# Two transformer layers on one core: attention blocks in another order, half 1's third stage on GpSimd inside the attention, half 0's second norm and router inside it too, and another order of VectorE at both hand-overs

## The reference

```python
x = x + two_graph_attention_layers(ctx_512, layernorm(x))        # adjacency from x
x = x + experts(layernorm(x))          # 8 experts, 2 per row, 256 -> 512 -> 256
x = x + (1 - gamma) * layernorm(x) + gamma * symmetric(sigmoid(sim) * top_76(sim))
h = layernorm(x)
r = rmsnorm(h, ln1)                                              # in layer L1_ffn
q, k, v = rope(r @ Wq), rope(r @ Wk), r @ Wv                     # 32 heads, 4 for k and v, of 128
y = h + (softmax(causal(q @ k.T / sqrt(128))) @ v) @ Wo
t = rmsnorm(y, ln2)
w = top 8 of 32 of sigmoid(t @ Wr) + bias, normalised scores
x = x + y + sum_e w[e] * (silu(t @ Wg[e]) * (t @ Wu[e])) @ Wd[e] + shared_expert(t)
```

## Time and profile before

| what | value |
|---|---|
| median of 3 runs (lowest to highest) | 1194.25 us (1194.03 to 1195.7) |
| the profiled execution | 1188.88 us |
| its span | 1187.1 us |
| TensorE busy | 1062.9 us, 90% of the span |
| VectorE busy | 876.8 us, 74% |
| ScalarE busy | 595.0 us, 50% |
| GpSimd busy | 381.0 us, 32% |
| mean granted clock | 0.922 of full |

### The profile page before, as it was taken

One profiled execution on the slowest core, in us unless ns is written; L12 is line 12 of the kernel. 1 busy time (PEld: TensorE's weight loads), 2 busy tenths in 40 slices (PEclk: granted clock), 3 DMA queues, 4 the chain that ended last, 5 costly groups with the idle time before them and its releaser, 6 DMA issues.

```text
span 1187.1 us, 20152 instructions
## 1 busy us (share of the span) xinstructions
PE 1062.9 (90%) x6074; PEld 857.5 (72%) x6074; DVE 876.8 (74%) x2615; ACT 595.0 (50%) x1564; POOL 381.0 (32%) x321
## 2 busy tenths in 40 slices
PE   3988887585999926899999999999998999999997
PEld 2555554352666615789999999999987788888887
DVE  5887888622777457987777777777786888888887
ACT  2656565232333314877777777776883222222221
POOL 2656564034000052533333333422330232333321
PEclk9877888557999967999999999999998999999999
DMA  9900000211111140111010101000010111111111
GB/s 266 351 1 1 1 1 2 64 36 58 45 45 45 40 155 0 41 41 37 2 45 2 37 4 29 2 1 1 1 41 1 41 42 51 48 44 53 40 53 35
DMA packets 55570, 53.58 MB, mean 45 GB/s; under 512 B 5520, under 2 KB 48976, under 8 KB 55488
## 3 DMA queue, kind: packets, MB, share of 16 engines
q1 hardware_dynamic: 52768, 47.27, 12.7%
q0 software_dynamic: 1536, 4.20, 1.1%
q10 hardware_dynamic: 1184, 1.11, 0.3%
HBM read 43.38 MB, written 9.18 MB: 44 GB/s over the span
## 4 chain that ended last, share of the span: by engine, by line
PE 78%; DVE 10%; ACT 5%; issue 3%; POOL 2%; DMA 1%; SPq 0%; DVEq 0%; ACTq 0%; POOLq 0%
PE bank L56 12%; PE bank L57 12%; PE bank L58 12%; PE bank L892 7%; PE bank L913 5%; PE bank L623 4%; PE bank L792 4%; PE bank L817 3%; PE bank L800 3%; PE bank L902 3%; PE bank L914 2%; PE bank L606 2%; DVE g_scale L1487 2%; PE bank L592 1%; PE bank L871 1%
## 5 line engine op out<-in xcount | busy, mean ns | idle before, releaser
L1367 POOL TENSOR_TENSOR rot_s<-swap,rq 128x512 f32<-128x512 f32 x64 | 88.5, 1383 | 199.1 <-ACT swap L1173 199.1
L1049 ACT ACTIVATE silu<-bank 128x512 f32<-128x512 f32 x66 | 39.5, 598 | 174.6 <-PE bank L58 174.6
L1865 DVE TENSOR_TENSOR o_ring<-bank,o_ring 128x256 fp32r<-128x256 f32 x128 | 54.3, 424 | 83.7 <-ACT o_ring L1202 83.0
L1186 ACT ACTIVATE prob<-prob,pmin 128x128 f32<-128x128 f32 (+1 forms) x256 | 113.3, 446 | 2.3 <-DVE pmin L1846 2.3
L892 PE MATMUL bank<-kv,norm 128*128 128x128 f32 (+1 forms) x512 | 106.0, 330 | 7.8 <-DVE norm L1839 7.8
L1676 DVE SCALAR_TENSOR_TENSOR xs<-bank,wt,xs 128x256 f32<-128x256 f32 x264 | 109.1, 476 | 0.1
L1315 POOL TENSOR_TENSOR gate_r<-gate_w,gate_r 128x256 fp32r<-128x256 f32 x31 | 36.4, 1173 | 178.7 <-ACT gate_r L1042 178.7
L1299 POOL TENSOR_SCALAR rest<-alpha 128x512 f32<-128x512 f32 x32 | 68.6, 2143 | 74.2 <-ACT alpha L987 72.7
L1202 ACT ACTIVATE o_ring<-bank 128x256 fp32r<-128x256 f32 x128 | 48.3, 378 | 80.1 <-PE bank L914 79.9
L56 PE MATMUL bank<-wo_r,o_ring 128*128 128x256 f32 x256 | 84.1, 329 | 0.0
L1858 DVE TENSOR_SCALAR prob<-prob,pinv 128x128 f32<-128x128 f32 (+1 forms) x256 | 78.2, 348 | 4.6
(11 more groups left out here) (285 smaller groups left out, 3125.0 us busy)
## 6 DMA issues: line engine op xcount, KB each, us to landing
gate_w<-in_Wg SPq DMA_DIRECT2D x33, 128.0 KB, 2.1
up_w<-in_Wu SPq DMA_DIRECT2D x33, 128.0 KB, 2.3
down_w<-in_Wd SPq DMA_DIRECT2D x33, 128.0 KB, 2.2
w_all<-in_w_gate SPq DMA_DIRECT2D x8, 512.0 KB, 10.7
w_all<-in_w_up SPq DMA_DIRECT2D x8, 512.0 KB, 10.3
w_all<-in_w_down SPq DMA_DIRECT2D x8, 512.0 KB, 10.7
wq_g<-in_Wq SPq DMA_DIRECT2D x4, 1024.0 KB, 5.2
wo_g<-in_Wo SPq DMA_DIRECT2D x4, 1024.0 KB, 5.4
```

The source lines that it names most:

```text
L1186: ins = act.activation(prob[:, u % 4, nt * P:nt * P + (nt + 1) * P], prob[:, u % 4, nt * P:nt * P + (nt + 1) * P], ACT.Exp, bias=pmin[:, u ...
L1367: pool.tensor_tensor(rot_s[:, m % 2].rearrange("p (b n) -> p b n", b=2), swap[:, m % 2].rearrange("p (b n) -> p b n", b=2), bcast(tab[:, 1 ...
```

## The change

1. The blocks come in the order of `ORDER`: (group, half) 0,0; 1,0; 0,1; 1,1; 2,0; 3,0; 2,1; 3,1. Half 1 is first needed in block 2, and half 0's last block is block 5. Loads and splits of weights follow that order; `wv_g` has two places; group 1's query weights are loaded under the sparse experts, `Wo`'s first part after the gathers of tile 3.
2. Half 1's third stage (tiles 4 to 7) goes to GpSimd inside the attention: the two weighted additions (`add_second`, four instructions each), the inverse roots by a power, the mixing (`mix_second`), the normalising; only the moments and the blend factors stay on VectorE. The turned rows of tiles 4, 5 and 6, 7 go into the bank of the next job, at iterations 3 and 11 (`ROWS_AT`).
3. All eight `residual` and all eight `add_x3` go to GpSimd; `sig` is scaled once on GpSimd under the sparse experts in place of `x3` on VectorE after them.
4. Half 0's second norm, its turning (iterations 107 and 110), logits (112), split (114) and router (116, 118) run inside blocks 6 and 7, in the banks of the jobs.
5. At the first hand-over VectorE gathers tile by tile and splits half 0 in two pieces; V's product begins after the first two tiles. At the start of the mixture `down(2)` comes before `gate_up(3)`, VectorE copies two of the four tiles of turned rows, and the router's parts of half 1 lie on both sides of `multiply(4)`.

```diff
+        ORDER = ((0, 0), (1, 0), (0, 1), (1, 1), (2, 0), (3, 0), (2, 1), (3, 1))
+        ROWS_AT = {3: (4, 5), 11: (6, 7)}
+        ROWS2_AT = {AU - 21: (0, 1), AU - 18: (2, 3)}
+        LOGITS_AT = AU - 16
...
         def turn_bank(t):
-            return Q_BANK[t % 2] if t < 4 else W_BANK[t % 2]
+            return (W_BANK[t] if t < 2 else bank[2 + t]) if t < 4 else Q_BANK[jobs_ahead(3 + 8 * (t // 2 - 2)) % 2][:, t % 2 * D:t % 2 * D + D]
...
+            sp.wait_ge(S["tok_in3"], 16 * K0)
             load_output(0)
...
                 down(1, 1)
                 for t in range(4, T):
                     turn2(t)
+                down(2, 2)
                 gate_up(3, 3)
-                down(2, 2)
                 logits(1)
...
                 def project(n, blk, i):
+                    for at, ts in ROWS_AT.items():
+                        if n == jobs_ahead(at):
+                            pe.wait_ge(S["normT_copied"], T + ts[1] + 1)
+                    for at, ts in ROWS2_AT.items():
+                        if n == jobs_ahead(at):
+                            pe.wait_ge(S["normT_copied"], 2 * T + ts[1] + 1)
+                    if n == jobs_ahead(LOGITS_AT):
+                        pe.wait_ge(S["rexp_done"], 2)
...
# ScalarE, behind copy_T(k - 2) and exps(k) of the same iteration
+                    for t in ROWS_AT.get(k - 1, ()):
                         scaled_copy(1, t, turn_bank(t))
+                    for t in ROWS2_AT.get(k - 1, {AU + 6: (4, 5)}.get(k, ())):
                         copy_rows2(t)
+                    if k == LOGITS_AT + 1:
                         exps_of_logits(0)
...
# GpSimd
+            def add_second(b, k):
+                ts = (NT * b, NT * b + 1)
+                done = 2 * NT * (b - 2) + NT * k
+                for t in ts:
+                    pool.wait_ge(S[f"tok_in{t}"], 16 * K0)
+                    pool.tensor_scalar(ytok[:, k, t, :], ytok[:, k, t, :], w_tok[:, k, t:t + 1], None, ALU.mult
+                                       ).then_inc(S["rest_scaled"], 1)
+                for j, t in enumerate(ts):
+                    pool.wait_ge(S["rest_scaled"], done + j + 1)
+                    pool.tensor_tensor(xs[:, t, :], xs[:, t, :], ytok[:, k, t, :], ALU.add).then_inc(S["rest_added"], 1)
...
+                if k in (-4, -3):
+                    add_second(3, k + 4)
+                for job, at in ((inverse_in, -4), (mix_second, -2), (inverse_out, 0), (normalise_second, 1)):
+                    if k in (at, at + 5):
+                        job(2 + (k - at) // 5)
+                if k in (9, 10, 11, 12, 26, 27, 28, 29):
+                    residual((9, 10, 11, 12, 26, 27, 28, 29).index(k))
+                if 0 <= k - (AU - 20) < 4:
+                    add_x3(k - (AU - 20))
...
# VectorE, in the loop over k
+                    for job, at in ((measure, -5), (mix_learned, -3), (measure_mixed, -1)):
+                        if k in (at, at + 5):
+                            job(2 + (k - at) // 5)
+                    if k == 15:
+                        split_activations(1, slice(512, 1024), 3)
+                    if k == AU - 14:
+                        split_activations(2, slice(0, 512), 4)
+                    if k in (AU - 12, AU - 10):
+                        router1(0, (k - (AU - 12)) // 2)
```

306 lines of the change are left out of this document (174 added, 132 removed).

## The result

The changed kernel takes 1205.01 us (median of 4 runs, 1202.68 to 1206.06) against 1194.97 of the kernel before on the same chip (4 runs, 1194.03 to 1195.70): ratio 1.0082, 95% interval 1.0064 to 1.0099. It is slower by 0.8%, 10.0 us; 0.6 us faster was forecast. The profiled execution took 1204.7, its span 1202.9.

What follows compares the result with a forecast made beforehand. TensorE was taken to bound steady attention, leaving gains only where it idled; 3.8 - 7.6 - 0.5 + 4.9 made it 0.6 us faster, a median of 1193.6 us. Own range 1190.5 to 1196.5; with rivals (1) and (2), 1186.5 to 1199.

Steps and rivals of the forecast that it cites:

- Hand-over until K's product: First hand-over: earlier gathers and V's product in halves let K's product start at 445.8 instead of 450.2, 4.4 us sooner.
- From K's product to a full pipeline: Hand-over's later part: despite GpSimd's long list, iteration 5 starts at 481.1 instead of 484.96; gain 3.8 us.
- I take 0.4: GpSimd's hand-over list: assumed 0.4 us per 128x256 TENSOR_SCALAR; at 1.07 the 3.8 gain becomes a 1.6 loss.
- New waits of PE: Full attention stretch: products at iterations 12, 108, 111 and 113 wait for ScalarE to clear their bank; loss 7.6 us.
- rival (1): Products at iterations 12, 108, 111, 113: ScalarE clears banks in time, 7.6 us come back, 1186.0 us; chance 0.2.
- Half 0's last stage: Blocks 6 and 7: split and router parts among products hold TensorE; loss 0.5 us, bounds gain 1.2 to loss 3.
- The start of the mixture: Expert mixture's start: reordering, shared copies, an unreduced clock and straddling router parts shorten TensorE's waits; gain 4.9 us.
- Rival (2): Hand-over: GpSimd slower than taken, TENSOR_SCALARs at 1.07 or rotations held; 5.4 us more, 1199.0 us; chance 0.2.
- rival (3): Mixture's start wins little, VectorE's work nearly unchanged and the clock still falling; 3.0 us less gain, 1196.6; chance 0.15.
- the rule against the change: VectorE beside GpSimd: two-SBUF-input VectorE instructions contend with GpSimd's SBUF reads; added GpSimd work can hold rotations, rarely in steady state.

Runs made afterwards that it cites:

- e2_half0_late: The changed kernel with half 0's second norm, logits, split and router put back to iterations 121 to 127; ratio 0.9999 to the kernel before.
- e8: The kernel before, with the loads of output and next query weights waiting for tile 3's gathers; ratio 0.9993 to the kernel before.
- e3: The changed kernel with the eight weighted additions of tiles 4 to 7 back on VectorE; 1198.45 us, ratio 1.0038 to the kernel before.
- e1: The changed kernel with ScalarE copying turned rows and taking the logits' exp before its other work of the iteration; 1193.97 us, ratio 1.0000 to the kernel before.
- e5: The changed kernel with the edits of e1, e2_half0_late and e3 together; 1184.81 us, ratio 0.9915 to the kernel before.
- e4: The kernel before with only the mixture start's new order and two tiles copied by VectorE; ratio 0.9991 to the kernel before.
- e7: e4 with half 1's four additions of x3 moved to GpSimd as well; ratio 0.9961 to the kernel before.
- e10: e5 with the mixing and normalising of tiles 4 to 7 on VectorE too; ratio 0.9955 to the kernel before.
- e12: e10 with both parts of the first output weights formed four iterations later; ratio 0.9936 to the kernel before.
- e6: e5 with half 1's split in two pieces of 256 columns, in iterations 14 and 15; ratio 0.9920 to the kernel before.

## Why the prediction was wrong

The chain, the four waits and the mixture's start were named rightly; the sum failed at one term above all, GpSimd's list at the hand-over, and by a smaller part at the router. In the prediction's order:

- **Hand-over until K's product: gain 4.4.** Measured 3.0, and 4.5 in e2_half0_late, where ScalarE's late copy is absent. The size was right. So was the reading of the loads, which held tile 0's gather (there at 3.3 us from the start, forecast 3.1), but taking them away brings nothing by itself (e8).
- **From K's product to a full pipeline: gain 3.8.** Here the sum failed, at "I take 0.4". The eight TENSOR_SCALARs took 1.05 each, the upper bound of that step (1.07), for which it had given a loss of 1.6. With the same program e2_half0_late has iteration 5 at +1.8 against before. In the changed kernel's profile it is 3.2, and 4.1 by iteration 10, with the late copy and a clock of 0.72 in iteration 4 and 0.81 in iteration 5 (e2: 0.80 and 1.00). Off by 7.9 in all, of which the price makes 5.2 (8 x 0.65). The mistake is one of choosing the row: both candidates stood in the earlier trace rows, and nothing in the trace said which the new instruction resembles. Taking four pairs of such instructions away with their additions won 8.5 us in e3, and 6.1 between e1 and e5, where the clock is alike.
- **New waits of PE: loss 7.6.** Measured 2.09 + 2.10 + 2.07 + 1.22 = 7.5, and e1 took them away by their named cause. This term was exact; rival (1) was wrong. Two things beside it I left out: half 1's split now lies in the full stretch (iteration 16 takes 3.67 instead of 2.36), and the clock can fall behind such a wait. From 10 to 22 the loss was 3.0, of which 2.1 had been counted.
- **Half 0's last stage: loss 0.5.** Its size was wrong. Iterations 115, 117, 118 and 119 lose 0.68 + 0.78 + 0.18 + 2.15 = 3.8; with the stalls taken out, 107 to 129 lost 8.6 - 5.4 = 3.2, the far bound of the step (3). I had spread VectorE's 86 idle us evenly, 0.8 an iteration, as if it could save them up; but the output sum that TensorE wants is made in the same iteration as the router part, and the wait for it is paid in full.
- **The start of the mixture: gain 4.9.** Measured 4.8, but by other shares: the order and the shared copies alone brought nothing (e4), the additions on GpSimd on top of them 3.2 (e7), with the fall behind the second wait in them, and the clock kept behind the first wait 1.6. Whether the change or its place in time kept it, no run shows. The total fitted partly by luck.

Sum: +4.1 + 3.0 + 8.6 - 4.8 = 10.9 us by the two profiles, against 10.0 by the runs. Rival (2), a slower GpSimd at 1.07, was what happened at its place, and it foresaw 1199.0. The other 6 us are the router's 2.7, the split, the late copy and the clock. Two slips in its figures change nothing of this: rival (1)'s 1186.0 lies outside the range that is said to reach to it, and the parts of rival (3) add up to 0.18, not 0.15.

On the rule against the change (the Trainium skill, SBUF — State Buffer, "Who interferes with whom"): the traces agree with it and more strongly than the steady-state median suggested. In e10 a 128x2 VectorE instruction took 1.22 and 1.30 us beside GpSimd's two-input ones, where its mean is 0.28 to 0.30 in the kernel before; and in e12 the second factor ended with another of GpSimd's instructions. The rule as the prediction puts it is about two inputs; the second factor, a TENSOR_SCALAR with one tensor and a column as scalar, was held too.

## What to carry to other kernels

- Work given to an idle engine has to be asked for twice: what is its price there, and who waits for that list during the few us in which it runs. In a stretch where every engine waits for another, GpSimd's idle time is not free; the best of these kernels gave it the mixing and the normalising and left the sums on VectorE.
- When a new tenant shares a bank with the pipeline, look where its reader stands in the reader's own list. Four waits of 1.2 to 2.1 us shrank to 0.2 or nothing by placing the copy first.
- If the trace offers two prices for an instruction that it does not hold, do not let the sum rest on the cheap one without a reason that the trace gives. Time a small edit in its own stage, counted from a point behind which the program is the same, since the whole time scattered by over 5 us either way. Read the granted clock of that stretch in both before the difference is called the edit's.

## What the runs showed of the hardware

- GpSimd's TENSOR_SCALAR of 128x256 with columns as scalars takes 0.96 to 1.37 us in the mean of its lines, with one operation (L1404, L1437) or two (L1454, L1448), more than its two-input addition of the same shape (0.72). With two constants an add-multiply of 128x512 took 0.66; what makes the difference no run here separates. By shape (groups of the changed kernel, GpSimd: count, busy us, mean ns):

```profile
L1454 POOL TENSOR_SCALAR xs<-sim,mv,rstd 128x256 f32<-128x256 f32 x8 | 9.8, 1224 | 0.0
L1404 POOL TENSOR_SCALAR ytok<-ytok,w_tok 128x256 f32<-128x256 f32 x8 | 8.3, 1046 | 0.0
...
L1410 POOL TENSOR_TENSOR xs<-xs,ytok 128x256 f32<-128x256 f32 x8 | 5.6, 718 | 0.0
L1448 POOL TENSOR_SCALAR norm<-sim,mv,rstd 128x256 f32<-128x256 f32 x4 | 5.5, 1370 | 0.0
...
L1437 POOL TENSOR_SCALAR xs<-xs,blend 128x256 f32<-128x256 f32 x4 | 3.8, 958 | 0.0
```

- A small VectorE instruction that began beside a two-input 128x512 instruction of GpSimd ended with it, within 0.03 us: 128x2 in 1.22 and 1.30 us (e10, e12). A longer one ran on: in e6 the subtraction of 128x512 ended 0.56 us behind GpSimd's low part, and took 1.65 instead of 0.69.
- The same product at the hand-over ran at a granted clock of 0.50 in some profiles and at 1.00 in others (K's product, e2 and e3), 1.3 us apart up to ScalarE's first swap.
- TensorE's granted clock fell to a mean of 0.61 to 0.67 over the 4 us behind a wait of 1.8 us in four executions, and stayed at 1.00 behind the same wait with the same work in eight others, at a price of 1.5 to 1.6 us. What decides it no run here showed; the four lay within 0.7 us of each other in their place behind the hand-over. The Trainium skill, TensorE: Matmul & The Clock Gate, "Part 1: The HAM clock gate", says that the gate's watch runs freely and is not tied to the kernel's start, so that one kernel can meet it differently from run to run; e10 and e12 agree with that as far as they go, two kernels and not one run twice. Open is also the cause of ScalarE's late copy, seen once, and of the 8 us of scatter ahead of the hand-over, which no kernel here was made to examine.
